# Group norm and self-attention over 16 images: the queries of both halves as one Strassen product of quarters, and a new order of an image's work

## The reference, cut to what matters

```python
# x: (16, 32, 32, 512) float32; wq, wk, wv, wp: (512, 512); 32 groups of 16 channels
xn = group_norm(x) * gamma + beta            # statistics over all 1024 tokens of an image
xf = xn.reshape(B, 1024, 512)
q = xf @ wq + bq
k = xf @ wk + bk
v = xf @ wv + bv
scores = einsum('bnc,bmc->bnm', q, k) * 512 ** -0.5
attn = softmax(scores, axis=-1)
out = einsum('bnm,bmc->bnc', attn, v) @ wp + bp + x
```

## Time and profile before

| | |
|---|---|
| median of 3 runs | 2149.33 us |
| the profiled execution | 2150.32 us |
| its span | 2148.6 us |
| PE busy | 2131.5 us (99%) |
| DVE busy | 1438.0 us (67%) |
| POOL busy | 811.4 us (38%) |
| ACT busy | 673.1 us (31%) |
| one image of the loop (1019.60 to 1150.65 us) | 131.05 us |

### The profile page before, as it was taken

How to read it: one execution, slowest core, us unless ns; L and a number is a source line. 1 busy time by engine, 2 the same in 40 slices (tenths; PEclk the granted TensorE clock), 3 DMA queues, 4 the chain that set the end, 5 groups by cost and what they waited for, 6 DMA issues and landing times.

```text
span 2148.6 us, 28179 instructions
## 1 busy us (share of the span) xinstructions
PE 2131.5 (99%) x9433; PEld 1765.0 (82%) x9433; DVE 1438.0 (67%) x2287; ACT 673.1 (31%) x1117; POOL 811.4 (38%) x479
## 2 busy tenths in 40 slices
PE   7999999999999999999999999999999999999999
PEld 6878888888888888888888888888888888888887
DVE  6885675847768475784856758566684767747555
ACT  3241322414233142331423324132341423314231
POOL 2444343433533334332443434334333343433431
PEclk9999999999999999999999999999999999999999
DMA  8003021120302103021030211302112030210201
GB/s 210 20 25 94 1 74 44 43 75 0 98 20 59 59 5 103 10 63 54 10 107 0 68 49 34 83 0 81 36 44 73 0 101 16 59 59 10 68 1 60
DMA packets 110267, 108.13 MB, mean 50 GB/s; under 512 B 8476, under 2 KB 74016, under 8 KB 110240
## 3 DMA queue, kind: packets, MB, share of 16 engines
q1 hardware_dynamic: 107984, 103.58, 16.7%
q10 hardware_dynamic: 2256, 4.20, 0.8%
HBM read 74.19 MB, written 33.55 MB: 50 GB/s over the span
## 4 chain that ended last, share of the span: by engine, by line
PE 97%; DVE 1%; DMA 1%; SPq 1%; ACT 0%; issue 0%; DVEq 0%
PE psum L892 22%; PE psum L894 22%; PE psum L893 22%; PE psum L980 11%; PE psum L982 11%; PE psum L981 11%; DMA score<-in_x_dram 1%; SPq L261 1%; DVE score L691 0%; PE psum L939 0%; ACT score L490 0%; DVE bn L597 0%; DVE v_lo L580 0%; DVE shift L685 0%; ACT v_hi L473 0%
## 5 line engine op out<-in xcount | busy, mean ns | idle before, releaser
L892 PE MATMUL psum<-t_hi,xn_hi 128*128 128x512 f32 x1024 | 399.8, 390 | 1.5 <-DVE v_lo L580 1.5
L894 PE MATMUL psum<-t_hi,xn_lo 128*128 128x512 f32 x1024 | 398.5, 389 | 0.0
L893 PE MATMUL psum<-t_lo,xn_hi 128*128 128x512 f32 x1024 | 398.5, 389 | 0.0
L980 PE MATMUL psum<-v_hi,pt_hi 128*128 128x512 f32 x992 | 385.9, 389 | 0.0
L981 PE MATMUL psum<-v_lo,pt_hi 128*128 128x512 f32 x992 | 385.9, 389 | 0.0
L982 PE MATMUL psum<-v_hi,pt_lo 128*128 128x512 f32 x992 | 385.9, 389 | 0.0
L343 POOL TENSOR_TENSOR x_res<-x_res,out_bias 128x512 f32<-128x512 f32 (+1 forms) x144 | 180.6, 1265 | 418.5 <-issue 222.9
L675 DVE TENSOR_TENSOR top_part<-top_part,score 128x512 f32<-128x512 f32 x192 | 169.6, 884 | 227.9 <-ACT score L485 226.2
L485 ACT ACTIVATE score<-psum 128x512 f32<-128x512 f32 x256 | 151.3, 599 | 464.3 <-PE psum L894 464.3
L365 POOL TENSOR_TENSOR total_part<-total_part,score 128x512 f32<-128x512 f32 x186 | 267.5, 1438 | 55.1 <-ACT score L490 42.1
L490 ACT ACTIVATE score<-score 128x512 f32<-128x512 f32 x256 | 157.3, 633 | 293.2 <-DVE score L691 293.2
(11 more groups left out here) (116 smaller groups left out, 3062.9 us busy)
## 6 DMA issues: line engine op xcount, KB each, us to landing
x_res<-in_x_dram SPq DMA_DIRECT2D x128, 256.0 KB, 2.9
out_dram<-x_res SPq DMA_DIRECT2D x128, 256.0 KB, 2.0
x_blk<-in_x_dram SPq DMA_DIRECT2D x240, 128.0 KB, 2.9
score<-in_x_dram SPq DMA_DIRECT2D x16, 128.0 KB, 8.2
w_q<-in_L_conv_wq_dram SPq DMA_DIRECT2D x1, 1024.0 KB, 5.6
w_k<-in_L_conv_wk_dram SPq DMA_DIRECT2D x1, 1024.0 KB, 8.2
w_v<-in_L_conv_wv_dram ACTq DMA_DIRECT2D x1, 1024.0 KB, 10.0
w_p<-in_L_conv_wp_dram ACTq DMA_DIRECT2D x1, 1024.0 KB, 13.6
```

The source lines that it names most:

```text
L892: nc.tensor.matmul(dst, s_hi_, m_hi_, start=n == 0, stop=False)
L893: nc.tensor.matmul(dst, s_hi_, m_lo_, start=False, stop=False)
L894: last = nc.tensor.matmul(dst, s_lo_, m_hi_, start=False, stop=n == len(pairs) - 1)
L980: nc.tensor.matmul(dst, hi[:, m, queries], v_hi[:, m, :], start=m == 0, stop=False)
```

## The change

**The product.** t = A' xn' is cut into quarters: A' in two by two blocks of 256x256, xn' in two by two blocks of 256 channels by 512 tokens. A Strassen-Winograd scheme forms the four quarters of t with 7 quarter products instead of 8. Each quarter product is two banks (`p` = 0, 1) of 2 x 3 = 6 matmuls (`block_product`), so t takes 14 x 6 = 84 matmuls where it took 96. The seven left operands (A11, A12, A22 and the sums S1 to S4) are made once in the setup, by POOL and ACT. The four sums of blocks of xn' are made anew for each image (`block_sums`, DVE), and split (`sum_hi_parts` on ACT, `sum_lo_part` on DVE). The products are joined partly in PSUM (a second product `adds` to a bank) and partly by DVE (`u2`, `u3`, `t_sum`) in `queries`.

**The order on PE** is now: v tiles 0 and 1, `queries` (both halves), all 16 score tiles, v tiles 2 to 7, all 8 output tiles. t of both halves exists at once, each half has its own score and probability buffers, and the buffers share space in another way. `pt_lo_parts` now waits for POOL's sums (`s_sum`), since the two halves no longer take turns.

**POOL.** `row_sum` stands straight before `top(b, 0)`, and `total_sum` of half 0, which now follows `root`, straight before `top(b, 1)`. Before each stands a `sem_inc` that holds the wait. **SP** loads all four quarters of the image after next between the stores of tiles 4 to 7.

The diff, cut to its core (blank lines left out):

```diff
-                sp.wait_ge(s_again[1], 16 * NI)
-                for q in range(2):
-                    sp.wait_ge(s_tr, q + 1)
+                sp.wait_ge(s_prod, PRODUCTS)
+                for q in range(NQ):
                     load_quarter(1, q)
...
                 for i in range(TH, NT):
+                    if images_left > 1:
+                        if i == TH:
+                            sp.wait_ge(s_o, b * NT + TH)
+                        load_quarter(b + 2, i - TH)
                     store_tile(b, i)
...
+                pool.wait_ge(s_rv, (n + 1) * KC)
+                pool.sem_inc(s_turn, 1)
                 nc.gpsimd.partition_all_reduce(row[:], row[:], P, ADD).then_inc(s_r, 1)
...
+            pool.wait_ge(s_seth, SET_A_LAST + 1)
+            block_sum(S1, a21, a22, ALU.add)
+            block_sum(S3, a11, a21, ALU.subtract)
             root(0)
-            pool.wait_ge(s_xl0, KC)
+            pool.wait_ge(s_as, 2)
+            block_sum(S2, ab_sum[:, S1], a11, ALU.subtract)
+            pool.wait_ge(s_as, 3)
+            block_sum(S4, a12, ab_sum[:, S2], ALU.subtract)
...
+            for at in (S1, S2, S3, S4):
+                block_lo(at, ab_sum[:, at])
...
+            pool.wait_ge(s_prod, PRODUCTS)
...
+                    row_sum(b)
...
                 totals(b, 0)
-                await_total_part(b, 0)
-                residual(b, 3, 0, C // 2)
-                total_sum()
                 if more:
                     root(b + 1)
+                await_total_part(b, 0)
+                total_sum()
                 await_top_part(b, 1)
-                residual(b, 3, C // 2)
                 top(b, 1)
+                if starts(b):
+                    for i in range(TH):
...
+                    pt_hi_parts(b, 1, 2 * j, 2 * j + 2, more)
+                    if more:
+                        xn_split(b + 1, j, j + 1)
                 if more:
...
+            def block_sums(n):
+                to = sums_of(n)
+                for i in range(4):
+                    if i == 0:
+                        one, two, at, op = quarter_block(x_t, 0, 1), quarter_block(x_t, 0, 0), (0, 0), ALU.subtract
...
+                    dve.wait_ge(s_u1, n * 2 + p + 1)
+                    dve.wait_ge(s_prod, done + 2)
+                    nc.vector.tensor_tensor(u2[:], BANK_6, u1[:], ALU.add).then_inc(s_u2, 1)
...
+                    dve.wait_ge(s_u2, n * 2 + p + 1)
+                    dve.wait_ge(s_prod, done + 4)
+                    nc.vector.tensor_tensor(u3[:], BANK_7, u2[:], ALU.add).then_inc(s_u3, 1)
+                    dve.wait_ge(s_u3, n * 2 + p + 1)
+                    dve.wait_ge(s_prod, done + 5)
+                    nc.vector.scalar_tensor_tensor(out=t_sum[1][:, 2 + p, :], in0=BANK_5, scalar=bias_1, in1=u3[:],
+                                                   op0=ALU.add, op1=ALU.add).then_inc(s_tc, 1)
...
+                    dve.wait_ge(s_prod, done + 6)
+                    nc.vector.scalar_tensor_tensor(out=t_sum[0][:, 2 + p, :], in0=BANK_7, scalar=bias_1, in1=u2[:],
+                                                   op0=ALU.add, op1=ALU.add).then_inc(s_tc, 1)
+                    dve.wait_ge(s_th, n * 8 + 4 * p + 2)
+                    lo_part(t_lo[1][:, 2 + p, :], t_sum[1][:, 2 + p, :], t_hi[1][:, 2 + p, :], s_tl)
+                    dve.wait_ge(s_prod, done + 7)
+                    nc.vector.scalar_tensor_tensor(out=t_sum[1][:, p, :], in0=BANK_5, scalar=bias_0, in1=u2[:],
+                                                   op0=ALU.add, op1=ALU.add).then_inc(s_tc, 1)
+                    dve.wait_ge(s_th, n * 8 + 4 * p + 3)
+                    lo_part(t_lo[0][:, 2 + p, :], t_sum[0][:, 2 + p, :], t_hi[0][:, 2 + p, :], s_tl)
+                    dve.wait_ge(s_th, n * 8 + 4 * p + 4)
+                    lo_part(t_lo[1][:, p, :], t_sum[1][:, p, :], t_hi[1][:, p, :], s_tl)
...
+                    dve.wait_ge(s_sum, (n * NH + h) * (NT - 1) + max(m, 1))
+                    lo_part(pt_lo[h][:, m, :], score[h][:, m, :], pt_hi[h][:, m, :], s_ptl)
...
+            dve.wait_ge(s_wide, 16 * 3)
+            dve.wait_ge(s_again[0], 16 * NI)
+            sum_products(0, KC)
             variance(0)
...
+            setup_lo_parts(SET_M, m_hi, m_lo)
...
                 for m in range(NT):
                     top_part_step(b, 1, m)
+                    if more and m == 3:
+                        group_variance(b + 1)
+                    if m > 1:
+                        pt_lo_parts(b, 0, m - 2, m - 1)
+                pt_lo_parts(b, 0, NT - 2, NT)
+                if more:
+                    variance(b + 1)
+                for m in range(2, NT - 1):
+                    v_lo_part(b, m)
+                    if more and m == 4:
+                        norm(b + 1)
+                totals(b, 0)
+                tile_shift(b, 1)
+                shifts(b, 1, 0, TH)
+                v_lo_part(b, NT - 1)
+                shifts(b, 1, TH, NT)
+                tile_out(b, 0)
+                for j in range(KC):
+                    pt_lo_parts(b, 1, 2 * j, 2 * j + 2)
...
+                        xn_lo_parts(b + 1, j, j + 1)
+                    if j:
+                        tile_out(b, j)
...
+                    block_sums(b + 1)
                 totals(b, 1)
...
+                    if more:
+                        sum_lo_part(b + 1, i - TH)
...
+            def block_product(dst, at, p, right_hi, right_lo, r, s, adds=False):
...
+                for k in range(2):
+                    left_hi, left_lo = ab_hi[:, at, k, chunk(p)], ab_lo[:, at, k, chunk(p)]
+                    nc.tensor.matmul(dst, left_hi, hi[:, k], start=k == 0 and not adds, stop=False,
+                                     skip_group_check=adds)
+                    nc.tensor.matmul(dst, left_hi, lo[:, k], start=False, stop=False, skip_group_check=adds)
+                    last = nc.tensor.matmul(dst, left_lo, hi[:, k], start=False, stop=k == 1,
+                                            skip_group_check=adds)
+                last.then_inc(s_prod, 1)
...
+                for p in range(2):
+                    if p:
...
+                    block_ready(A11, p)
+                    block_product(BANK_1, A11, p, xn_hi, xn_lo, 0, 0)
+                    if p:
+                        pe.wait_ge(s_u2, n * 2 + 1)
+                    else:
+                        pe.wait_ge(s_xsl, n * 4 + 1)
+                    block_ready(S2, p)
+                    block_product(BANK_6, S2, p, xs_hi, sums_lo, 1, 1)
+                    pe.wait_ge(s_u1, n * 2 + p + 1)
...
+                    block_product(BANK_1, A12, p, xn_hi, xn_lo, 1, 0, adds=True)
+                    if p:
+                        pe.wait_ge(s_tc, n * 6 + 2)
+                    else:
...
+                    block_ready(S3, p)
+                    block_product(BANK_7, S3, p, xs_hi, sums_lo, 0, 1)
+                    if p:
+                        pe.wait_ge(s_tc, n * 6 + 3)
+                    else:
...
+                    block_ready(S1, p)
+                    block_product(BANK_5, S1, p, xs_hi, sums_lo, 0, 0)
+                    pe.wait_ge(s_u3, n * 2 + p + 1)
+                    if p == 0:
+                        pe.wait_ge(s_xsl, n * 4 + 4)
...
+                    block_product(BANK_7, A22, p, xs_hi, sums_lo, 1, 0, adds=True)
+                    pe.wait_ge(s_tc, n * 6 + 3 * p + 1)
...
+                    block_product(BANK_5, S4, p, xn_hi, xn_lo, 1, 1, adds=True)
...
+                for i, k in enumerate((0, 2, 1, 3)):
+                    if h == m == 0:
+                        pe.wait_ge(s_tl, n * 8 + 2 * i + 1)
+                    nc.tensor.matmul(dst, xn_hi[:, k, chunk(m)], t_hi[h][:, k, :], start=i == 0, stop=False)
...
-                    pe.wait_ge(s_free, (n + 1) * SPLIT)
+                    pe.wait_ge(s_free, n * SPLIT + PLACE[("v", 0, NT - 2)] + 1)
...
+                    if i == 0 and m == NT - 1:
+                        pe.wait_ge(s_free, (n + 1) * SPLIT)
...
                 v_tile(b, 1)
+                queries(b)
                 for m in range(NT):
                     score_tile(b, 0, m)
-                for j in range(KC):
-                    t_chunk(b, 1, j)
+                for m in range(NT):
+                    score_tile(b, 1, m)
+                    if more and m == 2:
+                        group_sum(b + 1, 0, mv[:, :, 0])
+                    if more and m == 6:
+                        group_sum(b + 1, 1, dev[:])
                 for m in range(2, NT):
                     v_tile(b, m)
...
+                for i in range(NT):
                     out_tile(b, i, more)
```

642 lines of the change are left out of this document (350 added, 292 removed).

## The result

The changed kernel is slower: 2182.6 us, the median of four runs (2176.32 to 2192.97), beside 2149.1 for the kernel before. The ratio is 1.016 (95% interval 1.012 to 1.020). I had predicted 2166, with 2152 to 2182 as the forecast's own range and 2126 to 2198 as the wider one. Its runs lie 17 us apart, those of the kernel before 2. The profiled execution took 2178.84 us, its span is 2177.1.

What follows compares the result with a forecast made beforehand. PE, busy 99% of the span, was the bound; 2148.6 - 43.6 - 1.3 + 13.3 + 7.7 + 14 x (1.6 + 1.3) = 2165.3 us, 2166 in the runs; range 2152 to 2182, wider 2126 to 2198.

Steps and rivals of the forecast that it cites:

- The sign: Whether the whole kernel gets faster or slower: forecast slower, chance 0.59, against faster 0.31 and same 0.10.
- 192 matmuls: PE's matmuls for t, 12 fewer in each of 16 images at 0.227 us each: 43.6 us saved.
- image 0's wait in the old order: PE's wait for DVE in image 0 of the kernel before, said to go: 1.3 us saved.
- setup, to the first scores: Start of the kernel: first scores at 83.4 us, 13.3 us lost, bounds 5 and 20.
- rest of image 0: Image 0 after its first scores: maximum ready 6 us late, PE waits 7.7 us, bounds 1.6 and 12.
- wait A: PE in output tile 0 waits for the last v tile's lo part, behind half 1's reduced maximum: 1.6 us an image.
- wait B: PE at the first score tile waits for a lo part of t held by `row_sum`: 1.3 us an image.
- The switch rule: On POOL: 5.75 us between ordinary operation and reduce, 7.0 to 7.5 back, none between two reduces.
- DVE is the bound: Rival: DVE doesn't catch up in an image, PE also waits for `pt_lo` of half 1: 2195 us, chance 0.19.
- Which lock: DVE's lo part beside `row_sum`: held until 4.4 us after the reduce's start, not the skill's whole 6.1 us.
- The waits are covered: Rival: DVE keeps up and `row_sum` starts before 20 us, so the loop's waits vanish: 2125 us, chance 0.27.
- The switch stays: Rival: `sem_inc` counts as ordinary work on POOL, each pair of reduces keeps two switches, 13 us: 2350 us, chance 0.02.

Runs made afterwards that it cites:

- a1_vlo: The changed kernel with the lo part of the last v tile moved back ahead of totals and shift of half 1: 2184.7 us, ratio 1.016.
- b1_xn_behind: a3_both with DVE's four `xn_lo` of the next image behind the eight `pt_lo` of half 1, not one after each pair: 2133.1 us, ratio 0.992.
- c2_quarters_first: The changed kernel with SP issuing all sixteen loads of the next input ahead of the store of tile 4: 2169.1 us, ratio 1.009.
- b2_first_image: b1_xn_behind with four moves in setup and image 0 (variance, block sum S2, POOL's bias chain and residuals earlier): 2128.4 us, ratio 0.990.
- a3_both: The changed kernel with the last v tile's lo part early and `row_sum` waiting for the last lo part of t: 2161.8 us, ratio 1.0057.

## Why the prediction was right, step by step

The sign was right. My time lies 16.6 us under the median, which is 0.6 us above the forecast's own range and well inside the wider one. Of the steps, against the span of 2177.1:

| term | predicted | measured |
|---|---|---|
| 192 matmuls | -43.6 | -43.5 (128.33 for 131.05 us, 16 times) |
| image 0's wait in the old order | -1.3 | -1.3 |
| setup, to the first scores | 13.3 (83.4) | 14.5 (84.57) |
| rest of image 0 | 7.7 | 15.2 |
| wait A, images 1 to 14 | 14 x 1.6 | 14 x 1.75 |
| wait B, images 1 to 14 | 14 x 1.3 | 12.7 in four images |
| what follows a wait (clock), and small ones, images 1 to 14 | 0 | 7.3 |
| not placed | 0 | -0.9 |
| sum | 16.7 | 28.5 |

The loop came out closer than its terms deserve. B and the small losses together make 20.0 us where I had 18.2 for B alone, and an image takes 131.5 us on average where I had 131.2. But no image took that: most took 130.2 to 130.5, and four 133.2 to 137.1. The 5.5 us that B had too much were made good by 7.3 that I hadn't foreseen, which is luck.

**Wait A** in the loop held link by link: adds end at 68.3 (68.6 measured), variance 73.4 (73.9), maximum 86.0 (86.6), v_lo 91.2 (91.3), the wait 1.6 (1.75). The switch rule held too: 6.1 us ahead of a reduce, nothing between two. What the step lacked is what lies behind A. The same chain delays the adds of half 1 and with them `pt_lo`, which DVE serves between `xn_lo`; a1_vlo shows wait C at once. I had `pt_lo` as a rival, "ready only 1 us early", but as a sign that DVE is the bound; b1_xn_behind shows it to be a matter of order.

**Wait B** had the right mechanism, and the start of `row_sum` was mis-sized. I put `row_sum` at 21 to 22 us and allowed "perhaps 1 us" for the quarters of x. SP's issue takes 2.6 us between two stores, the loads went out at 9.4 where I had 6.9, and `row_sum` came at 25.7, mostly behind the cliff that I had put at 26 and that is at 25.4. So B was not 1.3 in every image but 2.5 to 3.8 in those four where the reduce was a little early. c2_quarters_first, with the quarters out of the way, came near what I predicted: `row_sum` at 18.7 to 21.5 us, and 0.5 to 1.0 of wait in nine images.

**Which lock.** The held lo part of image 1 ended 1.05 us before the reduce did; taking off its own 0.68 us, it was let go 4.6 us after the reduce began, 4.4 in the earlier trace rows. The held ones of all loops of the changed kernel were let go after 4.4 to 4.8 us, and each ended 1.05 us before its reduce. The Trainium skill ("SBUF — State Buffer", the two physically separate sides) has the loser blocked for the whole instruction; by that it would have been let go after 6.3 us here, and the trace disagrees. A lo part that reads PSUM isn't held (0.69 us in the earlier trace rows), nor is one that began before the reduce (0.68 us at 757.22, above).

**The setup** came out by its own steps: v tiles at 51.86 (51), first scores 84.6 (83.4), clock 0.50 about 51 us. **Image 0** is the term that was too small, and it was made of the wrong parts. I had put all of its 7.7 us into wait A, behind a late maximum; A was 2.7. The rest was waits of 4.0 and 2.6 us for the statistics of image 1, 1.4 for a `pt_lo`, and two stretches of 3.4 us at clock 0.50 behind such waits, 1.7 us each. I had followed only the chain of the maximum. `first_row` and the transposes stand ahead of the statistics on DVE, and POOL's bias chain and reduces run beside them. That these make the waits is argued, and shown only in part: in b2_first_image, where the bias chain starts earlier and three other things move too, the first of them falls to 1.0 and the second grows to 3.4.

**The rivals.** "The waits are covered", 2125, is what the same matmuls do in a better order: 2128. "DVE is the bound" is refuted by b1_xn_behind, with 111.9 us of DVE work in a 128.33 us image and no wait. I had counted 108 us of work by volume; the changed kernel's common image has DVE busy for 115.1, the time lost beside POOL included. "The switch stays" did not come.

## What to carry to other kernels

Taking matmuls out of a kernel in which PE never waits gives back exactly their pace, but only as long as every engine's order still meets its times. Here 43.5 us of matmuls went out, and waits with what follows them cost 44.5 us in the loop and the new setup and image 0 another 30. The places of one `v_lo` and of one reduce made the loop's waits, that of four `xn_lo` the wait behind them, and three small moves brought the loss of 33 us to a gain of 16; the start is what is left. When one wait goes, look at what the same chain feeds next; and where a cost has a cliff, make the order explicit with a wait instead of leaving it to the time of a transfer.

## What I had not expected of the hardware

- A reduce that starts about 1 us earlier made a kernel 22 to 30 us slower (2212.9 against 2190.6 and 2182.6), and leaving out most of four block sums of DVE in each image or moving loads changed the time mainly through that start.
- A subtraction held by that reduce ended 1.05 us before the reduce's end, whether it had been held for 3.0 us (image 2 of the changed kernel) or for 4.4 (image 11).
- A pause of PE of about 2 us was followed in five of fourteen images of one execution by 3.4 us at half the clock (0.55 in the window), 1.7 us of further loss; pauses of 1.5 us, in every image of a3_both, were followed by none in the loop. In the changed kernel one of four pauses of 2.5 to 3.8 us was followed by such a stretch, twice as long.
- Moving a subtraction out from beside POOL's adds saved DVE nothing in all. `xn_lo` (128x1024) fell from 1.76 us on average to 1.21, but the `pt_lo` that came to stand there rose, and DVE's busy time stayed (1817.0 and 1819.7 us).
